# Attention stage: the output projection moves ahead of the first weighted values, and the two value projections of the second half are split between two loop bodies

## The reference

```python
sh_msa, sc_msa, g_msa, ... = split(silu(c) @ W_mod + b_mod, 6)
h = layernorm(x) * (1 + sc_msa) + sh_msa
q, k, v = split(h @ W_qkv, 3)              # 16 heads of 64
attn = softmax(q @ k.T * 64 ** -0.5)       # for each head, 128 x 128
x = x + g_msa * (concat_heads(attn @ v) @ W_out + b_out)
```

## Time and profile before

| | us |
|---|---|
| median of 3 runs (lowest to highest) | 737.24 (734.24 to 740.25) |
| profiled execution | 738.05 |
| its span, first to last instruction | 736.6 |
| busy in the span: PE / DVE / ACT / POOL | 659.2 / 468.8 / 477.6 / 337.4 |
| weight loads of PE | 570.5 |
| mean granted TensorE clock | 0.952 of full speed |

### The profile page before, as it was taken

One profiled execution on the slowest core, in us unless ns is written; L12 is line 12 of the kernel. 1 busy time (PEld: TensorE's weight loads), 2 busy tenths in 40 slices (PEclk: granted clock), 3 DMA queues, 4 the chain that ended last, 5 costly groups with the idle time before them and its releaser, 6 DMA issues. The chain is left out here.

```text
span 736.6 us, 17167 instructions
## 1 busy us (share of the span) xinstructions
PE 659.2 (89%) x5496; PEld 570.5 (77%) x5496; DVE 468.8 (64%) x1010; ACT 477.6 (65%) x1707; POOL 337.4 (46%) x390
## 2 busy tenths in 40 slices
PE   5789999999999999999999985999789898988874
PEld 5578888888888888888888874899667777777763
DVE  4456666666765666666676555576266776768672
ACT  4767877887797797788779771688344444444541
POOL 1334354445444435344444344466426564655642
PEclk9989999999999999999999999799789999999995
DMA  7212012021011102202201210234111111111100
GB/s 230 57 25 54 16 53 60 7 61 53 25 42 53 51 17 53 58 9 60 53 20 40 54 41 18 71 112 126 54 47 29 52 37 50 39 53 42 30 15 29
DMA packets 57757, 36.77 MB, mean 50 GB/s; under 512 B 15536, under 2 KB 54480, under 8 KB 57728
## 3 DMA queue, kind: packets, MB, share of 16 engines
q1 hardware_dynamic: 54480, 27.80, 13.8%
q0 software_dynamic: 3248, 8.61, 3.8%
HBM read 30.05 MB, written 6.34 MB: 49 GB/s over the span
## 5 line engine op out<-in xcount | busy, mean ns | idle before, releaser
L477 POOL TENSOR_TENSOR p<-p,p_rsum 128x512 f32<-128x512 f32 x128 | 130.4, 1040 | 126.3 <-DVE p_rsum L793 126.3
L694 ACT ACTIVATE p<-banks,neg_max 128x128 f32<-128x128 f32 x512 | 182.4, 393 | 0.1
L672 ACT ACTIVATE wide<-banks 128x512 f32<-128x512 f32 x128 | 78.3, 612 | 73.9 <-PE banks L530 71.3
L694 ACT ACTIVATION_READ_ACCUMULATOR p<-banks,neg_max 128x1 f32 x512 | 120.2, 235 | 0.0
L804 DVE COPY oT<-banks 128x512 f32<-128x512 f32 x64 | 44.1, 689 | 78.3 <-PE banks L581 78.3
L566 PE MATMUL banks<-ident,p 128*128 128x128 f32 x512 | 75.4, 281 | 17.5 <-DVE oT L804 15.3
L786 DVE TENSOR_REDUCE neg_max<-banks 128x8 f32<-128x1024 f32 x64 | 77.6, 1212 | 17.7 <-PE banks L555 16.3
L528 PE MATMUL banks<-xT_hi,w_qkv_hi 128*128 128x256 f32 x256 | 83.9, 328 | 4.0 <-DVE w_qkv_lo L196 2.5
L566 PEld LDWEIGHTS banks<-ident,p 128*128 128x128 f32 x512 | 56.2, 142 | 26.4 <-issue 17.3
L555 PE MATMUL banks<-wide 64*128 64x128 f32 x1024 | 74.4, 285 | 0.2 <-ACT wide L672 0.2
L529 PE MATMUL banks<-xT_lo,w_qkv_hi 128*128 128x256 f32 x256 | 74.1, 290 | 0.0
(11 more groups left out here) (147 smaller groups left out, 1474.5 us busy)
## 6 DMA issues: line engine op xcount, KB each, us to landing
early<-in_mask SPq DMA_DIRECT2D x16, 220.0 KB
early<-in_mask SPq DMA_DIRECT2D x80, 44.0 KB
x_in<-in_x SPq DMA_DIRECT2D x16, 128.0 KB, 2.2
x_gb<-in_x SPq DMA_DIRECT2D x16, 128.0 KB, 2.2
gate_msa<-rows_scratch SPq DMA_DIRECT2D x16, 128.0 KB, 3.0
gate_b_out<-rows_scratch SPq DMA_DIRECT2D x16, 128.0 KB, 3.4
f_x_in<-x_scratch SPq DMA_DIRECT2D x16, 128.0 KB, 2.4
f_x_res<-x_scratch POOLq DMA_DIRECT2D x16, 128.0 KB, 2.8
```

Of the source, the lines that this page charges most:

```text
L477: pool.tensor_tensor(p[:, par, heads, :], p[:, par, heads, :], p_rsum[:, par, heads].unsqueeze(2).broadcast_to([128, 4, T]), ALU.mult).the ...
L672: act.activation(dst, proj_ps[k % 2], ACT.Copy).then_inc(proj_saved[k % 2], 1)
L694: act.activation(p[:, par, m, :], s_ps[par][:, e, j, :], ACT.Exp, bias=neg_max[:, par, 4 * e + j:4 * e + j + 1], accum_out=p_sum[:, par, m ...
```

## The change

`project_out(i)` goes from behind `probs_v(i, 0)` to ahead of it. The V1 projections are separated: item 1's stays in the body, now between the two transposes of unit 0; item 0's becomes task 14, in bank 0, and is computed at the end of the preceding body, after V0[1] and ahead of `probs_v(i, 3)`; its save becomes the last thing in ACT's body. For body 0 it is computed ahead of the loop. `task_count` is adapted so that 14 counts as an even task.

```diff
-    V1, XT, OUT, QK0, QK1, V0 = ((0, 1), 2, 3, (4, 5, 6, 7), (8, 9, 11, 12), (10, 13))
+    V1, XT, OUT, QK0, QK1, V0 = ((14, 1), 2, 3, (4, 5, 6, 7), (8, 9, 11, 12), (10, 13))
     def in_body(i, k):
         if i < 0:
-            return k not in V1 + (OUT,)
+            return k not in (V1[1], OUT)
         if i == PAIRS:
             return k == OUT
-        return k in V1 or (i > 0 if k == OUT else i < PAIRS - 1)
+        return k == V1[1] or (i > 0 if k == OUT else i < PAIRS - 1)
     def task_count(i, k):
-        done = [... for t in range(k % 2, TASKS, 2) if in_body(j, t)]
+        done = [... for t in range(2 - k % 2, TASKS + 1, 2) if in_body(j, t)]
     def probs_v(i, unit):
             if half:
-                wait_saved(pe, i, V1[b])
+                wait_saved(pe, i - 1 + b, V1[b])
     # tensor body
             scores(i, 2, i - 1, QK1)
             turn_p(i, 0, 0)
+            project_v(i, V1[1], 1, 1)
             turn_p(i, 0, 1)
-            project_v(i, V1[0], 1, 0)
-            project_v(i, V1[1], 1, 1)
             if nxt:
                 turn_x(i)
-            probs_v(i, 0)
             if more(i, -1):
                 project_out(i)
+            probs_v(i, 0)
...
                 project_v(i, V0[1], 0, 1)
+                project_v(i, V1[0], 1, 0)
             probs_v(i, 3)
     # tensor, ahead of the loop
+        project_v(-1, V1[0], 1, 0)
         run_bodies(pe, body)
     # scalar body
             save_turned(i, 0)
-            save_v(i, V1[0], 1, 0)
             save_v(i, V1[1], 1, 1)
...
                 save_v(i, V0[1], 0, 1)
+                save_v(i, V1[0], 1, 0)
     # scalar, ahead of the loop
+        save_v(-1, V1[0], 1, 0)
         run_bodies(act, body)
```

More of the change, by code:

```diff
@@ L401, in task_count @@
             return (i - 1) * (TASKS // 2) + task_count(1, k)
-        done = [(j, t) for j in range(-1, i + 1) for t in range(k % 2, TASKS, 2) if in_body(j, t)]
+        done = [(j, t) for j in range(-1, i + 1) for t in range(2 - k % 2, TASKS + 1, 2) if in_body(j, t)]
         return sum(1 for task in done if task <= (i, k))
```

## The result

| | us |
|---|---|
| after: median of 5 runs (lowest to highest) | 753.64 (753.62 to 754.55) |
| before, measured beside it: median of 5 runs (lowest to highest) | 734.29 (733.89 to 740.25) |
| ratio after / before, 95% interval | 1.0242 (1.0206 to 1.0278) |
| profiled execution after, and its span | 753.64, 752.2 |
| mean granted TensorE clock | 0.958 of full speed |

The change makes the kernel 2.4% slower. The ratio is taken over the runs and not over the medians, which are 19.4 us apart; the runs of the kernel before scatter by 6 us. Against the median of 737.24 us shown ahead of the prediction the ratio is +17.8 us; the forecast was +17.5.

A forecast was written before the change was run, and what follows sets the result against it. PE was taken to bound the attention stage. 15 tails (+21.0), 15 heads (-1.8) and body 0's head (-1.7) gave +17.5 us on the 737.24 median: 755 us, range 744 to 763.

The forecast's parts named there:

- Offsets of the head: Body's start, scores 2 (T' is its new start) to turn_p(1,0) at +10.46: gains 0.12 us a body.
- The tail: End of the preceding body: V1[0] waits 0.63 us for bank 0, and probs_v(3) moves by +1.40 us.
- A body: An inner body of the attention stage goes from 26.41 to 27.69 us.
- Body 0: First body, without project_out: turn_p(1,0) comes 1.7 us earlier; V1[0]'s 0.79 us is hidden in the front.
- PE-bound: Rival, 6%: only PE's stream and old holes count, project_out goes earlier, the 0.69 us hole vanishes; -15, 722 us.
- The holes trade places: Rival, 8%: one new wait bites, the other is covered; about 0 per body, 735 to 740 us.
- Tail hidden: Rival, 7%: bank 0 free when V0[1] ends, tail costs 0.79 us, head as forecast; +8.4, 746 us.
- The clock: Rival, 4%: new PE holes lower the clock in each body; 25 us more, 780 us.
- The room that the weight loads seem to leave: By LDWEIGHTS busy, 15% of a body, 4.05 us, would be room to hide work; the sum does not use it.

The follow-up runs named there:

- three edits of order: Changed kernel with ACT saving V1[1] ahead of save_turned(0) and QK1[3] ahead of unit 5's exps, and DVE's sum_cells behind save_oT(0): body 25.84 us, ratio to before 0.9787.

## Why the prediction held

The forecast was 755 us, +17.5 on the median; measured were 753.64 us and a ratio worth +17.8. Term by term:

- **Offsets of the head.** From T' = 223.19: V1[1] +1.51 (forecast +1.51), turn_p(0,1) +2.30 (+2.30), turn_x +2.73 (+2.72), save_turned +2.93 (+3.00), save of v +3.43 (+3.49), project_out +4.07 (+4.12), cast +6.64 (+6.72), sum_cells +7.77 (+7.85), residual +8.76 (+8.83), oT +9.56 (+9.63), turn_p(1,0) +10.39 (+10.46). The error of 0.07 us is the start of save_turned: I had put it 0.70 us behind the last four transposes, read from a group of eight, and it is 0.63 (225.49 to 226.12). The head gained 0.19 us instead of 0.12. In front of project_out PE stood 0.96 us and not 1.2: the start was right, and PE was ready later than the +2.9 of the forecast.
- **The tail.** +1.48 us instead of +1.40: V1[0] waited as forecast and started 1.37 us behind V0[1] (forecast 1.33); the group with its restart took 0.90 us instead of 0.86.
- **A body.** 27.70 us against 27.69: the two small errors cancel.
- **Body 0.** turn_p(1,0) came 2.1 us earlier (37.26 instead of 39.36), forecast 1.7. That this is close is in part luck. The front brought the first transposes 0.67 us earlier (28.74 instead of 29.41); counted from them the gain is 1.43 us. And the save that was left out is not all of that: in the profile of the kernel before the granted clock was 0.50 from 31.1 to 34.7 us, while most of the two V1 projections ran, and in that of the changed kernel it was 1.00 there, which the forecast did not look at. V1[0] ahead of the loop was hidden as forecast: the wait before the first transposes is 0.63 us instead of 1.85. Over the whole stage the last store is 17.2 us later, forecast 17.5.
- **The rivals.** PE-bound: refuted by the project_out move alone, which gave 0. The holes trade places: they did in that kernel, where 0.3 us moved from the transposes to project_out for nothing, but V1[0]'s tail came on top. Tail hidden: it would have cost 0.90, not 0.79; the kernel with V1[0] behind the weighted values shows it. The clock: it is 1.00 in inner bodies with holes of up to 0.96 us, so this did not happen.
- **The room that the weight loads seem to leave.** The Trainium skill (Perfetto Trace Analysis, Identifying the Most-Contended Engine) takes LDWEIGHTS busy for the measure. It is 22.38 of 27.70 us in the changed kernel (81%), 22.36 of 26.41 before (85%), 22.52 of 26.00 in the one with three edits of order (87%). It ranks these kernels rightly, and so does matmul busy (93%, 97%, 100%). What it didn't give is a place to hide V1[0]'s work: none of its 0.9 us was hidden in the tail, and in that last kernel no matmul waits though the weight loads leave 13%.

What was not foreseen is how much body 0 gains in the experiments with DVE's new order, below. It did not touch the forecast, since the change leaves that order alone.

## What to carry to other kernels

When an instruction waits, look for every chain that reaches it and note how far apart they end: here the residual was held by project_out and by an unrelated reduction ahead of it in DVE's queue, within 0.1 us, so moving one alone brought 0.00 or 0.10 us a body, and moving both 0.40. A producer moved forward on one engine paid here only when the save that frees its buffer moved forward in the other engine's hand-written order as well (0.45 us, and with the reduction out of the way 1.3 us). Work moved into a neighbour body is not free there: ask when the bank it takes is freed, in the queue of the engine that frees it.

## What the runs showed of the hardware

**A long hole costs more than its length.** In body 0 of the kernel before and of the changed one turn_p(1,0) waits 3.0 and 3.6 us behind sum_cells. Windows of the kernel before, where the last column but two is the granted clock:

```profile
35.00:40.00 5.00, 2.00 (x25) 1.67 (x22) 2.88 (x5) 2.51 (x11) 1.31 (x1) 0.82 0.20 54
40.00:45.00 5.00, 5.00 (x26) 5.00 (x25) 2.08 (x3) 2.30 (x7) 2.61 (x3) 0.50 0.19 38
```

The changed kernel:

```profile
35.00:40.00 5.00, 2.74 (x13) 2.77 (x14) 4.48 (x6) 0.75 (x2) 3.40 (x3) 0.64 0.33 83
40.00:45.00 5.00, 5.00 (x38) 4.70 (x37) 0.11 (x2) 4.06 (x15) 0.51 (x1) 0.68 0.04 10
```

And the changed kernel with oT ahead of sum_cells:

```profile
35.00:40.00 5.00, 4.49 (x44) 3.87 (x42) 3.77 (x5) 4.12 (x14) 2.86 (x2) 1.00 0.31 76
40.00:45.00 5.00, 5.00 (x51) 4.34 (x51) 3.22 (x9) 4.43 (x18) 3.50 (x6) 1.00 0.09 17
```

Behind the hole the clock stands at its lower level, 1.2 GHz, until about 45 us in the kernel before and 43 us in the changed one, and from 40 to 45 us PE gets through 26 and 38 recorded matmuls instead of 51; without the hole the clock stays at 2.4 GHz. All seven profiles with a hole of 3.0 to 3.8 us there show the fall, the five with oT ahead of sum_cells, in which PE waits 0.4 us at most at that place, don't. How long the clock stayed low after PE had started again differs, from 2.9 to 5.9 us.

What the hole cost is read from the last two kernels. From the first transposes of body 0 to the start of body 1's scores 2 it is 28.29 us with it (28.74 to 57.03) and 22.77 us without (29.41 to 52.18), 5.5 us less. 3.7 us of these are the hole and 1.7 us the slower stretch behind it. The first store gains another 0.80 us inside body 1, where the residual no longer waits for sum_cells, and loses 0.67 us to the front: together the 5.65 us.

The Trainium skill (TensorE: Matmul & The Clock Gate, What's actually happening) says that the clock is halved after idling; these traces agree for the holes of 3.0 to 3.8 us and show no fall for repeated holes of up to 1 us. Stops between these lengths occur in the front: in the kernel before, with and without oT ahead of sum_cells, the clock was also at its lower level from about 31 to 34.7 us, behind waits of 1.85 and 2.01 us before the first transposes, and it was not in five kernels whose wait there was 0.63 to 1.43 us. In four others it fell at about 25 us, behind waits of 1.77 to 2.61 us; it didn't there in the changed kernel behind one of 1.72, nor in the kernel with V1[0]'s move alone behind one of 2.24. What decides it in between is left open.

**What repeats and what does not.** Inner bodies repeat to 0.04 us. The front and the stages behind attention don't: the first store differs by 1.45 us between the kernel before and the one with project_out early, and the 1.46 us are there already at the start of body 1's scores 2 (57.54 and 56.08), up to which the two have the same instructions; and the stretch from the last store to the end takes 297.0 to 302.9 us in twelve profiled executions of the same code, for instance 297.4 at a mean granted clock of 0.91 (the three edits of order) and 302.9 at 0.88 (the kernel before with oT ahead of sum_cells). Why the clock there differs is left open. It is the reason why a body's length settles what the ratio of the runs leaves within half a per cent.
